# Turning rows by 32x32 block transposes on VectorE and quadrant copies on ScalarE, in place of TensorE transposes

## The reference, cut to what matters

```python
x = L0_attn_x                                   # [4, 512, 512] f32
x = x + 0.5 * ffn(layernorm(x), w_gate, w_up, w_down)
x = x + attn(layernorm(x), W, lam_logit, eta, gamma, beta)
x = x + 0.5 * ffn(layernorm(x), w_gate, w_up, w_down)

def ffn(x, w_gate, w_up, w_down):               # 512 -> 2048 -> 512
    return (silu(x @ w_gate.T) * (x @ w_up.T)) @ w_down.T

def attn(x, W, lam_logit, eta, gamma, beta):    # the "mixer"
    z = x @ W.T
    m = scan over time: m[t, k] = sigmoid(lam_logit[k]) * m[t-1, k] + z[t]
    return gamma * layernorm(z + sum_k eta[k] * m[k]) + beta
```

## Time and profile before

| | |
|---|---|
| median of 3 runs | 1043.59 us (1042.96 to 1044.24) |
| the profiled execution's own time | 1043.7 us |
| its span in the profile | 1041.9 us |
| TensorE busy | 1035.8 us (99%) |
| VectorE busy | 644.8 us (62%) |
| ScalarE busy | 363.6 us (35%) |
| GpSimd busy | 115.9 us (11%) |

### The profile page before, as it was taken

One profiled execution on the slowest core, in us unless ns is written; L12 is line 12 of the kernel. 1 busy time (PEld: TensorE's weight loads), 2 busy tenths in 40 slices (PEclk: granted clock), 3 DMA queues, 4 the chain that ended last, 5 costly groups with the idle time before them and its releaser, 6 DMA issues.

```text
span 1041.9 us, 12733 instructions
## 1 busy us (share of the span) xinstructions
PE 1035.8 (99%) x4672; PEld 857.2 (82%) x4672; DVE 644.8 (62%) x973; ACT 363.6 (35%) x607; POOL 115.9 (11%) x127
## 2 busy tenths in 40 slices
PE   9999999999999999999999999999999999999998
PEld 8888888887878888888887888888888888888887
DVE  7855666569687777856749877785665333333342
ACT  6645454533423322222533332232243322222311
POOL 3123332120200200010003020001100000000000
PEclk9999999999999999999999999999999999999999
DMA  5688867677666554648645764553676665566266
GB/s 202 242 320 314 306 243 252 222 232 243 232 222 227 177 174 165 198 145 269 219 162 192 246 202 142 182 181 132 221 224 220 212 202 182 182 195 208 76 193 208
DMA packets 61517, 217.89 MB, mean 209 GB/s; under 512 B 6160, under 2 KB 15376, under 8 KB 53776
## 3 DMA queue, kind: packets, MB, share of 16 engines
q1 hardware_dynamic: 60880, 216.03, 61.4%
q10 hardware_dynamic: 576, 1.05, 0.3%
HBM read 170.92 MB, written 46.14 MB: 208 GB/s over the span
## 4 chain that ended last, share of the span: by engine, by line
PE 94%; DVE 4%; DMA 1%; issue 1%; ACT 0%; DVEq 0%; ACTq 0%
PE ps_b L1409 7%; PE ps_a L1409 7%; PE ps_a L1411 7%; PE ps_a L1410 7%; PE ps_b L1411 7%; PE ps_b L1410 7%; PE ps_d L1411 6%; PE ps_d L1409 6%; PE ps_d L1410 6%; PE ps_c L1411 6%; PE ps_c L1409 6%; PE ps_c L1410 6%; PE aux L1411 3%; PE aux L1409 3%; PE aux L1410 3%; DVE rows L1110 1%
## 5 line engine op out<-in xcount | busy, mean ns | idle before, releaser
L932 DVE TENSOR_TENSOR tmp<-tmp,ps_c 128x512 f32<-128x512 f32 x59 | 40.4, 685 | 150.3 <-PE ps_c L1411 150.3
L1409 PE MATMUL ps_a<-xt,gu 128*128 128x512 f32 x304 | 118.8, 391 | 0.0
L1411 PE MATMUL ps_a<-xt,gu 128*128 128x512 f32 x304 | 118.4, 389 | 0.0
L1410 PE MATMUL ps_a<-xt,gu 128*128 128x512 f32 x304 | 118.3, 389 | 0.0
L1409 PE MATMUL ps_b<-xt,gu 128*128 128x512 f32 x286 | 112.3, 393 | 0.4 <-ACT tmp L538 0.3
L1410 PE MATMUL ps_b<-xt,gu 128*128 128x512 f32 x286 | 111.4, 389 | 0.0
L1411 PE MATMUL ps_b<-xt,gu 128*128 128x512 f32 x286 | 111.4, 389 | 0.0
L1409 PE MATMUL ps_d<-dn,hid 128*128 128x512 f32 x256 | 99.8, 390 | 0.0
L1411 PE MATMUL ps_d<-dn,hid 128*128 128x512 f32 x256 | 99.6, 389 | 0.0
L1410 PE MATMUL ps_d<-dn,hid 128*128 128x512 f32 x256 | 99.6, 389 | 0.0
L1409 PE MATMUL ps_c<-xt,gu 128*128 128x512 f32 x236 | 92.2, 391 | 0.1
(11 more groups left out here) (203 smaller groups left out, 2033.4 us busy)
## 6 DMA issues: line engine op xcount, KB each, us to landing
dn<-dn_kept SPq DMA_DIRECT2D x112, 512.0 KB, 3.4
gu<-gu_kept SPq DMA_DIRECT2D x46, 1024.0 KB, 5.1
gu<-gu_kept SPq DMA_DIRECT2D x46, 768.0 KB, 5.4
gu_kept<-gu SPq DMA_DIRECT2D x14, 1024.0 KB, 4.3
gu_kept<-gu SPq DMA_DIRECT2D x14, 768.0 KB, 4.2
dn_kept<-dn SPq DMA_DIRECT2D x16, 512.0 KB, 5.1
h_t<-w_ffn_in SPq DMA_DIRECT2D x18, 256.0 KB, 4.7
x_tok<-w_ffn_in SPq DMA_DIRECT2D x18, 256.0 KB, 5.0
```

What stands on the lines that cost most here:

```text
L932: dve.tensor_tensor(dst, u3s(si), p5_bank(si)[:, :], ALU.add).then_inc(c22_done, 1)
L1409: pe.matmul(dst, a_hi, b_hi, start=start, stop=False, skip_group_check=chained)
L1410: pe.matmul(dst, a_hi, b_lo, start=False, stop=False, skip_group_check=chained)
L1411: return pe.matmul(dst, a_lo, b_hi, start=False, stop=stop, skip_group_check=chained)
```

## The change

`turn_x` for phases 1 to 3 and all `turn_z` go from TensorE (24 + 16 units, 160 transposes). The same units are now turned in two steps. `blocks_x` and `blocks_z` (VectorE) turn the 32x32 blocks of a unit, each within its own quadrant of 32 partitions, into `x_turn` or into free units of `hid1`. Then ScalarE moves four units at a time: copy q of 16 takes the blocks of token quadrant i = q // 4 and feature quadrant j = q % 4 from partitions 32i to those of feature quadrant 32j, a copy of 32 partitions x 512 elements. So eight copies 128x512 from a bank become 32 copies 32x4x4x32 from SBUF.

```diff
+            def blocks_x(k, r):
+                if r == 0:
+                    dve.wait_ge(p3_done, upto(16 * k - 1))
+                dve.wait_ge(row_x_ready, 8 * k + r - 3)
+                dve.transpose(by_block(x_turn[:, r, :], True), by_block(row_x(k, r))).then_inc(x_blocks_turned, 1)
...
+            def place_x(k, l, q):
+                if q == 0:
+                    act.wait_ge(x_blocks_turned, 8 * (k - 1) + 4 * l + 4)
+                    act.wait_ge(lo0_ready, 16 * k)
+                act.copy(to_quadrant(tmp[:, 4 * l:4 * l + 4, :], q // 4, q % 4),
+                         from_quadrant(x_turn[:, 4 * l:4 * l + 4, :], q // 4, q % 4)).then_inc(placed_x, 1)
...
+                        first, after = ((0, 0, 2, 5, 8, 12, 16, 20, 24, 28, 32) + 6 * (32,))[m:m + 2]
+                        for q in range(first, after):
+                            place_x(k, q // 16, q % 16)
...
                 if op == T1:
-                    dve.wait_ge(placed_x, 8 * k + 8)
+                    dve.wait_ge(placed_x, 32 * k + 8)
...
                 copy_u3(g)
                 copy_u3(u)
+                if beside:
+                    places_z(p, 0, 0, 4)
                 hi0(u, 0)
                 if beside:
-                    place_z(p, 2)
+                    places_z(p, 0, 4, 6)
                 silu_of(g, "22")
                 if beside:
-                    place_z(p, 3)
+                    places_z(p, 0, 6, 10)
                 silu_of(g, "21")
                 hi0(u, 1)
+                if beside:
+                    places_z(p, 0, 10, 13)
                 silu_of(g, "12")
+                if beside:
+                    places_z(p, 0, 13, 16)
...
-                    if p < PH - 1 and 2 <= m < 6:
-                        turn_x(p + 1, 2 * m - 4)
-                        turn_x(p + 1, 2 * m - 3)
```

More of the change, by code:

```diff
@@ L62, in sem @@
             return ctx.enter_context(nc.semaphore(name))
+        with nc.sbuf_tensor("xt_front", [P, 5, 4, tokens], F32), \
+                nc.sbuf_tensor("x_turn", [P, tiles * 2, tokens], F32) as x_turn:
+            pass
         xt = sb("xt", [P, 7, 2, 2, tokens], F32R)
@@ L143, in p5_bank, with turn_bank, turn_of_z, by_block @@
             return ps_d[2] if si == 1 else ps_c
[L145 to L149, removed]
+        def turn_bank(r):
+            return first_turn_ps[r]
         def row_z(v):
-            return zw[:, v % 2, :].bitcast(F32)
+            return zw[:, v % 2, :].bitcast(F32) if v < 4 else hid1[:, 4 + v, :]
+        def turn_of_z(v):
+            return hid1[:, 8 + v, :]
+        def by_block(unit, turned=False):
+            if turned:
+                return unit.rearrange("p (j c r) -> p j c r", j=4, c=DT)
+            return unit.rearrange("p (c j r) -> p j c r", c=DT, j=4)
+        def from_quadrant(turned, i, j):
+            return turned[32 * i:32 * i + 32, :, j * P:(j + 1) * P].rearrange("p s (c t) -> p s c t", c=DT)
+        def to_quadrant(feature_rows, i, j):
+            return feature_rows[32 * j:32 * j + 32, :, :].rearrange("p c (s i t) -> p i s c t", s=ST, i=4)[:, i]
         scan_sum = zw[:, 0, :].bitcast(F32)
@@ L644, in zw_hi_of, with place_z, places_z @@
                 act.copy(zw[:, 0, :], rows[:, j % 2, :]).then_inc(zw_hi, 1)
[L646 to L655, removed]
+            def place_z(p, l, q):
+                if q == 0:
+                    act.wait_ge(z_blocks_turned, 8 * (p - 1) + 4 * l + 4)
+                    if p == 1 and l == 0:
+                        act.wait_ge(gub_lo, made(17))
+                    wait(act, zlo_ready, 8 * (p - 1) + 4 * l)
+                act.copy(to_quadrant(h_t, q // 4, q % 4),
+                         from_quadrant(hid1[:, 8 + 4 * l:12 + 4 * l, :], q // 4, q % 4)).then_inc(placed_z, 1)
+            def places_z(p, l, q0, q1):
+                for q in range(q0, q1):
+                    place_z(p, l, q)
             def hi_total(p, j):
@@ L716, in _ @@
             raw_hi_odd(0)
-            place_x(0, 0)
-            place_x(0, 1)
+            place_first(0)
+            place_first(1)
             raw_hi_even(1)
-            place_x(0, 2)
-            place_x(0, 3)
+            place_first(2)
+            place_first(3)
             raw_hi_odd(1)
@@ L732, in _ @@
             for r in range(4, 8):
-                place_x(0, r)
+                place_first(r)
             hi0(1, 0)
@@ L777, in _ @@
                     copy_p1(g)
+                    if beside and si == 8:
+                        places_z(p, 1, 12, 16)
                     if p == 0:
@@ L783, in _ @@
                         hi0(g - 1, 1)
-                    if beside and si == 7:
-                        place_z(p, 4)
                     copy_u2(g)
                     if beside and si == 7:
-                        place_z(p, 5)
+                        places_z(p, 1, 0, 2)
                     if up:
@@ L1044, in norm_x @@
                 if k > 0:
-                    dve.wait_ge(turned_x, 8 * k + r - 1)
+                    wait(dve, x_blocks_turned, 8 * (k - 1) + (r - 1 if r >= 2 else 0))
                 if r < 2 and k in (2, 3):
@@ L1265, in first_quad @@
                 if beside:
-                    norm_z(p, 0)
-                    norm_z(p, 1)
+                    for v in (0, 1):
+                        norm_z(p, v)
+                        blocks_z(p, v)
                 c11(u)
-                if beside:
-                    norm_z(p, 2)
                 gated11(u)
                 if beside:
-                    norm_z(p, 3)
+                    for v in (2, 3):
+                        norm_z(p, v)
+                        blocks_z(p, v)
                 c22(g)
@@ L1324, in window @@
                 for m in range(16):
-                    if m == 0:
+                    if m == (4 if p < PH - 1 else 0):
                         for q in range(ST):
@@ L1626, in turn_x @@
                 last.then_inc(turned_x, 1)
-            def turn_z(p, v):
-                n = 8 * (p - 1)
-                pe.wait_ge(row_z_ready, n + v + 1)
-                if v == 0:
-                    pe.wait_ge(y1_added, 4 * p)
-                if v == 1:
-                    pe.wait_ge(placed_x, 8 * p + 8)
-                if v in (2, 3):
-                    pe.wait_ge(placed_z, n + v - 1)
-                if v >= 4:
-                    pe.wait_ge(placed_z, n + v)
-                ps, row = turn_z_bank(v), row_z(v)
-                for c in range(DT):
-                    last = pe.transpose(ps[:, c * P:(c + 1) * P], row[:, c * P:(c + 1) * P], ident[:, :])
-                last.then_inc(turned_z, 1)
             def mix(p, s):
@@ L1676, in _ @@
             for r in range(4):
[L1677 removed]
+                turn_first(r)
                 if r in KEEP:
@@ L1705, in first_quad @@
                 g, u = SETS * p, SETS * p + 1
-                beside = p in (1, 2)
                 prod1(g)
```

150 lines of the change are left out of this document (61 added, 89 removed).

## The result

The changed kernel takes 1065.29 us (median of 6 runs, 1062.76 to 1065.69) against 1043.48 us (1042.96 to 1044.24, 6 runs): a ratio of 1.0203, 95% interval 1.0189 to 1.0216. It is slower by 21.8 us where 8 us less was forecast. Two of the six runs took 1062.8 and 1063.1 us, at a granted clock of 0.991 and 0.990 over the whole run, the other four 1065.1 to 1065.7 us at 0.987 to 0.988. The profiled execution has a span of 1063.6 us, against 1041.9.

The account below looks back on a forecast made before the run. TensorE, busy 1035.8 us (99% of the span), bounds the kernel. Gains of 0.4 + 1.9 + 2.0 (windows) + 0 (quads) + 3.8 (sets 7) = 8.1 us take 1043.7 to 1036 us; range 1032 to 1053.

Parts of the forecast that it names:

- The turns removed: TensorE's turns taken out of three windows, two quads and two sets 7: 18.5 us gained if nothing else moved.
- I take 0.52 us a copy: ScalarE's quadrant copies: 0.52 us from start to start, overlapping like the trace's casts; forecast 1032 to 1040 us, chance 0.41.
- first rival: ScalarE's copies do not overlap as start partitions change: 0.1 us more each, sum -8.1 us, 1052 us; chance 0.35.
- its own sign of being wrong: Stated signs that the prediction is wrong included copies taking longer than 0.57 us, where gain and loss cross.
- The upper bound of 0.62: ScalarE's quadrant copy: 0.62 us if each starts only when the last has ended.
- The block transpose: VectorE's 128x512 transpose: 0.69 us, 1.18 with its norm; first four units turned 7.4 us after TensorE's first down1 (W).
- The windows: Phases 1 and 2: VectorE's add_y1 ends at W + 45.2, TensorE waits 1.7 us; 1.9 to 2.0 us gained each.
- Phase 0's window: Weight casts behind the last copy delay t_of by 2.4 us; add_y1 ends at W + 47.7, 0.4 us gained.
- The first quad: Phases 1 and 2, from the first product (Q): prod6 of set 2 waits 2.5 us, scans set the pace, 0 gained.
- that just holds: First quad: ScalarE's silu21 done at Q + 18.5, TensorE wanting it for set 2 at Q + 19.0.
- Sets 3 to 8: Phases 1 and 2: added norms, transposes and copies hidden; set 7's 1.92 us come out whole, twice: 3.8 us gained.
- TensorE's clock, put at nothing: TensorE's clock was found full (1.00) in the windows before; the sum has no term for it.

Follow-up runs that it names:

- experiment 7: Kernel before, with the mixer's second half and four of eight units per window turned by blocks, window order rewritten on three engines: 1035.31 us, ratio 0.9915.
- experiment 4: Kernel before, with only the second half of the mixer's rows turned by blocks and no turns in set 7: 1040.13 us, ratio 0.9967.
- experiment 1: Changed kernel with all quadrant copies on partitions 0 to 31, so they overlap; output not the reference's: 1037.84 us, ratio 0.9943.
- experiment 6: Changed kernel with add_y1 ahead of the last two lo_x, and also the quad's last three mixer copies behind copy_p1 of set 2: 1046.79 us, ratio 1.0027.
- 5: Changed kernel with VectorE's four add_y1 at each window's end ahead of the last two lo_x: 1051.33 us, ratio 1.0066.
- experiment 2: Changed kernel with only the copies' input quadrant changing in phase 0's window, only the output's in phase 1's, neither in phase 2's: 1050.75 us, single run.
- 3 (both): Changed kernel with unread 128x128 matmuls filling TensorE's five long waits: 28 at each, 1068.67 us, ratio 1.0242; 14 at each, 1055.23 us, ratio 1.0105.

## Why the prediction was wrong

- **The turns removed, 18.5 us.** Right as far as runs tell it: four turns in a window gave 1.9 and 1.8 us in phases 1 and 2 (experiment 7; forecast price 0.45 us a unit), four in set 7 gave 1.9 and 1.6 (experiment 4).
- **"I take 0.52 us a copy".** This is the step that failed, and the larger part of the miss (17.6 of 29.8 us, below). It is 0.64 us from start to start, and the same for a cast beside a copy. The prediction had this as its first rival at 0.35, and put against it that "every run of ScalarE in the trace overlaps"; those rows all begin on partition 0 and could not speak against it. Copies slower than 0.57 us were its own sign of being wrong. The upper bound of 0.62 was itself slightly short, since 0.02 us lie between end and start.
- **The block transpose, 0.69 us.** It took 0.71, with its norm 1.2 a pair; the first four units came at W + 7.5 (7.4 forecast).
- **The windows.** The chain named (32 copies, `t_of`, `hi_x`, `lo_x`, `add_y1`) is right: with overlapping copies the windows came within 0.3 us of the forecast (experiment 1; in phase 1 by some luck, since there TensorE lost its time at waits for weights in mid-window, 1.0 us the longest, and had none left at the end). With held ones 40 x 0.12 = 4.8 us are added. The rival had 40 x 0.1 = 4.0.
- **Phase 0's window.** The idle time of 3.4 us does not follow from the prediction's own sum, which gives 47.7 - 43.5 = 4.2 us less 0.6 for weights. The forecast had the weight casts delay `t_of` and so `add_y1`, but not that `d1_lo` for step 12 stands behind the same two subtractions. `d1_lo` starts at 247.57, and TensorE waits 2.7 us for it in the changed kernel. It seems to cost nothing of its own: `add_y1` comes late by VectorE's queue alone, and TensorE would have waited the longer for it. No run shows this by itself. The kernel with overlapping copies has no such wait (the longest for `d1_lo` is 0.2 us) and a window of 47.9 us.
- **The first quad.** `prod6` of set 2 waits 2.3 us with overlapping copies (2.5 forecast), 3.4 with held ones, and silu21 comes 0.9 us late ("that just holds" no longer held). That the scans behind it take everything was too strong: with the wait shorter by 2.0 us and some eight matmuls fast again (1.6 us), the stage was shorter by 2.4 of these 3.6 us (experiment 6 beside 5, phase 1).
- **Sets 3 to 8, 3.8 us gained.** Right: 3.6 us by themselves (experiment 4), with held copies.
- **What was missing: TensorE's clock, put at nothing.** The prediction found it full in the kernel before and priced an idle microsecond at one microsecond. Behind the long waits it costs more: at 292.23 it was 3.4 us of idle time and then some 2.4 us more for 12 matmuls 0.43 instead of 0.23 us apart. The Trainium skill ("TensorE: Matmul & The Clock Gate", part on the clock gate) says that the clock follows how busy TensorE has been and falls to half after it has been idle; the trace agrees, with 0.50 granted from 292.2 to 298.0 us, behind 3.4 us of idle time.

The whole account, in spans: the forecast's 8.1 us gained would be 1033.8. The kernel with overlapping copies has 1036.0, of whose miss of 2.2 us some 1.5 are seven slow matmuls behind its 2.4 us wait in phase 0 (Q to W is 222.3 us in phase 1, with them, and 220.7 in phase 2, without). Held copies bring it to 1053.6 with the waits filled: 17.6 us more, or 19.1 beside a kernel without those seven, where the rival had 16.2. The fallen clock adds 10.0: 1063.6. The rival "copies do not overlap" (1052) was right in mechanism: in spans it is 1050.0, 3.6 us short of the kernel with filled waits and 13.6 short of the changed one.

## What to carry to other kernels

Before work is moved to an engine in pieces on other partitions, price a piece by its full duration from end to end, unless a row shows two such pieces overlapping; rows that all begin on the same partition are no evidence (here 0.52 us taken, 0.64 measured). Count a long idle stretch of TensorE as more than itself (here five of 3.3 to 3.4 us cost 10 us more between them), and put what the next product waits for ahead of work that is needed later: moving two `lo_x` behind `add_y1` in each of three windows gave 14 us. A trade between engines need not be all or nothing: four of eight units of a window and the second half of the mixer's rows by blocks, in an order written for it, fit under the other work and gain 8 us, where all of them lose 22.

## What the runs showed that I had not expected

- ScalarE started an instruction only after the last had ended when the start quadrant of its input or of its output differed from the last one's: 0.64 for 0.52 us, each side alone (experiment 2).
- Idle time and what followed, in the changed kernel and the kernels of experiments 1, 2, 3 (both), 5 and 6: after 3.3 to 3.4 us, 9 waits of 9 were followed by matmuls 0.43 us apart (5 to 12 in a row); after 2.1 to 2.7 us, 5 of 11; after up to 1.4 us none. The same wait at the same place of the program is once followed by slow matmuls and once not: 2.31 us for `copy_p1` in both phases of experiments 1 (none slow) and 2 (8 and 7 slow), and some 2.65 us for `d1_lo` in phase 0. What decides between these stays open. The slow stretch does not always begin at the first matmul: at 819.07, behind 3.30 us, the first matmul that holds the next for 0.43 us is the one at 820.65, 1.6 us later.
- A filler, one f32 matmul of 128x128, appears as two records and takes 0.23 us of TensorE (28 of them 6.4 us), as much as a product's matmul of 128x512 on f32r parts.
